# Splitting one projection of a slot around the values' transposes in a two-layer delta-rule attention kernel

## What is computed

```python
mixed = x @ W_qkv;  z = x @ W_z                    # 16 key heads, 32 value heads, 128 wide
mixed = silu(causal_conv4(mixed))                  # 4 taps per channel
q, k, v = split(mixed);  q, k = l2norm(q), l2norm(k)
def step(S, (qt, kt, vt, gt, bt)):                 # over 512 positions
    S = S * exp(gt)
    u = (vt - kt . S) * bt
    S = S + outer(kt, u)
    return S, qt . S
o = rms_norm(o) * silu(z)                          # second layer: gate first, then the norm
y = o @ W_out
```

## Time and profile before

| | |
|---|---|
| median of 3 runs | 4766.57 us (4763.95 to 4771.02) |
| the profiled execution, its own time | 4774.79 us |
| its span | 4773.0 us |
| PE busy | 4393.9 us, 32596 products |
| DVE busy | 3868.8 us |
| ACT busy | 3005.2 us |
| POOL busy | 1009.3 us |
| DMA, mean | 89 GB/s |

### The profile page before, as it was taken

How to read it: one execution, slowest core, us unless ns; L and a number is a source line. 1 busy time by engine, 2 the same in 40 slices (tenths; PEclk the granted TensorE clock), 3 DMA queues, 4 the chain that set the end, 5 groups by cost and what they waited for, 6 DMA issues and landing times. The chain is left out here.

```text
span 4773.0 us, 93590 instructions
## 1 busy us (share of the span) xinstructions
PE 4393.9 (92%) x32596; PEld 3619.4 (76%) x32596; DVE 3868.8 (81%) x8126; ACT 3005.2 (63%) x9834; POOL 1009.3 (21%) x1252
## 2 busy tenths in 40 slices
PE   5899948999999999999959999299999999999998
PEld 3578736888888888888845877288888888888887
DVE  5938987888888888888851599788888888888887
ACT  1146636777777777777721666267777776767675
POOL 0014421122221212212100344021212122221211
PEclk8999978999999999999979999599999999999999
DMA  1035642232222223223210556222322222322222
GB/s 57 16 96 172 185 129 87 83 85 77 83 80 83 80 78 83 78 82 89 65 31 7 148 176 194 88 80 81 86 77 80 77 83 77 83 79 83 73 83 66
DMA packets 580414, 422.57 MB, mean 89 GB/s; under 512 B 392808, under 2 KB 476312, under 8 KB 579502
## 3 DMA queue, kind: packets, MB, share of 16 engines
q1 hardware_dynamic: 563566, 408.20, 29.4%
q0 software_dynamic: 16384, 8.42, 1.0%
HBM read 296.24 MB, written 120.16 MB: 87 GB/s over the span
## 5 line engine op out<-in xcount | busy, mean ns | idle before, releaser
L1232 DVE SCALAR_TENSOR_TENSOR conv_l<-mix_l,taps_l,conv_l 128x512 f32<-128x512 f32 x1152 | 869.1, 764 | 62.7 <-ACT conv_l L1051 21.9
L854 PE MATMUL pj_l<-x_high,w_high_l 128*128 128x512 f32 x1280 | 574.5, 449 | 160.5 <-ACT w_high_l L1060 160.5
L1435 POOL TENSOR_TENSOR fac_l<-den_l,powers 128x4 f32<-128x4 f32 x256 | 258.5, 1012 | 1622.5 <-DVE den_l L1356 1621.1
L1198 ACT ACTIVATE Z_l<-gb_l 128x128 f32<-128x128 f32 x1024 | 266.6, 288 | 433.1 <-PE gb_l L1014 433.0
L854 PE MATMUL pj_l<-x_high,w_low_l 128*128 128x512 f32 x1280 | 519.7, 406 | 2.6
L854 PE MATMUL pj_l<-x_low,w_high_l 128*128 128x512 f32 x1280 | 514.0, 402 | 0.0
L637 POOL DMA_DIRECT2D own_dram<-key_kkS_l x512 | 296.0, 585 | 925.5 <-ACT key_kkS_l L509 915.2
L1023 PE MATMUL gb_l<-wo_l,gT_l 128*128 128x256 f32 x2048 | 480.0, 384 | 0.0
L1023 PEld LDWEIGHTS gb_l<-wo_l,gT_l 128*128 128x128 f32 x2048 | 372.6, 190 | 69.7 <-ACT Z_l L1198 25.6
L1366 DVE SCALAR_TENSOR_TENSOR x<-gb_l,fac_l,x 128x256 f32<-128x256 f32 x1024 | 412.9, 476 | 13.6 <-POOL fac_l L1435 4.0
L854 PEld LDWEIGHTS pj_l<-x_high,w_high_l 128*128 128x128 f32 x1280 | 243.2, 190 | 219.0 <-ACT w_high_l L1060 160.8
(11 more groups left out here) (204 smaller groups left out, 10588.5 us busy)
## 6 DMA issues: line engine op xcount, KB each, us to landing
rows_l<-rows_dram SPq DMA_DIRECT2D x128, 1024.0 KB, 5.6
k_dram<-kT_l SPq DMA_DIRECT2D x128, 256.0 KB, 2.3
kk_dram<-key_kkS_l SPq DMA_DIRECT2D x128, 256.0 KB, 2.4
kq_l<-k_dram SPq DMA_DIRECT2D x128, 256.0 KB, 3.3
kkS_l<-kk_dram SPq DMA_DIRECT2D x128, 256.0 KB, 5.9
w_raw_l<-in_wx SPq DMA_DIRECT2D x32, 640.0 KB
lane_k_l<-own_dram SPq DMA_DIRECT2D x32, 512.0 KB, 4.1
t_dram<-lane_t_l SPq DMA_DIRECT2D x14, 1024.0 KB, 4.9
```

The source lines that it names most:

```text
L854: ins = nc.tensor.matmul(pj_bank(c, t), wt[:, k, t, :], xt[:, k, :, at], start=(k == 0 and n == 0), stop=(k == KD - 1 and n == 2))
L1198: ins = nc.scalar.activation(Z[:, g, bank(b)], gb[:, 0, g, bank(b)], ACT.Square, accum_out=ss_o[:, g, b:b + 1])
L1232: ins = nc.vector.scalar_tensor_tensor(out, mix[:, t, :, i:i + P], wt(i), out, ALU.mult, ALU.add)
L1435: nc.gpsimd.tensor_tensor(fac[:, g, :], den[:, g, :], m.powers[:, 1, :], ALU.pow).then_inc(fac_ok[g], 1)
```

## The change

In each slot that has it, the second half (k = 1) of projection 0 moves from ahead of the values' transposes to behind them, ahead of the outputs' transposes. It is the same six products into the same bank. The prologue's projection (L1034, L1035) stays as it is.

```diff
                     if it < KHEADS * CHUNKS - 2:
                         project(*following(nh, ncn), 0, 0, False)
-                        project(*following(nh, ncn), 0, 1, False)
                     if not last:
                         values_token_major(nh, ncn)
+                    if it < KHEADS * CHUNKS - 2:
+                        project(*following(nh, ncn), 0, 1, False)
                     for g in range(GROUPS):
```

## The result

| | before | after |
|---|---|---|
| median, 5 runs each | 4769.52 us | 4793.64 us |
| lowest to highest | 4763.95 to 4771.02 | 4787.42 to 4795.86 |
| ratio, 95% interval | | 1.0050 [1.0039, 1.0062] |
| span of the profiled execution | 4773.0 | 4788.6 |

The kernel is slower by 24.1 us. I had forecast 21.9.

The account below looks back on a forecast made before the run. PE, 92% busy, was taken to set slot length except where it waits for DVE in c = 2. Terms +21.3 and +0.6 gave +21.9 us; on the 4766.57 base, 4788.5 us forecast, range 4777 to 4797.

Parts of the forecast that it names:

- c = 3: 30 slots, 15 per layer: V stays put, the half's 0.71 us is not hidden before the outputs' transposes; +21.3 us.
- c = 0 and c = 1: 64 slots: V arrives before the first half ends, so values start 0.71 us earlier and outputs start unchanged; cost 0.
- c = 2, second layer: V falls inside the second half, but the outputs' transposes wait 0.50 us for the first gate anyway; cost 0.
- c = 2, first layer: First group's outputs' transposes 0.51 us later, hidden by two covers; taken as 0, at most 15 x 0.51 = 7.7 us.
- the first cover: First layer: output projection still waits for its gate; late ACT squares (1557.59) just precede the product needing them (1557.70).
- The border: One extra entry into a projection per slot, 124 in all: 0.005 us each, +0.6 us; at most 3.7 us.
- The exposed weight load: Rival: each extra entry into a projection exposes a 0.19 us weight load, 23.6 us more, 4812 us; chance 0.03.
- The clock: Rival: PE's longer idle time in 30 slots drops its clock to 1.2 GHz, another 21 us, 4810 us; chance 0.01.

## Why the prediction was right

**What bounds the kernel, and c = 3.** Right. V did not move with PE, the wait ahead of the values grew to 0.86 us, the outputs came at 1.64 behind the values, and DVE, ACT and the next slots moved along. The term was 30 x 0.71 = 21.3 us; the table above gives 10.5 + 10.6 = 21.1 and the run with c = 3 alone 21.0.

**c = 0 and c = 1.** Right: 0.00 us in 64 slots.

**c = 2, second layer.** Right: the first gate still sets the start of the outputs' transposes (V + 1.69 after, V + 1.68 before), and V to V is unchanged.

**c = 2, first layer.** This term was mis-sized: I took 0 out of a range up to 7.7 us, and it is 3.5. The delays were as worked out (squares 0.49 us late, sums of x 0.33), and the first cover held: the output projection was not late. The step that failed is "DVE is some 0.3 to 0.5 us late into the c = 3 slot, where it has 0.91 us to wait anyway". The 0.91 us lie at L1252, 7 us behind the W blocks that PE takes from DVE first, and there PE had slack for only about half of the delay. By then ACT, which ends the wait at L1252, is late with PE: DVE comes 0.30 us later than before and still waits 0.83 us. I had asked where DVE would catch up and not who waits for it before that.

**The border.** Forecast 0.005 us each. From V to the outputs' transposes of c = 0 it is 0.007 us more than before in both layers, of c = 1 0.003 at most. The exposed weight load, which the rule of the Trainium skill that the prediction names would have given ("TensorE: Matmul & The Clock Gate", "Part 3: Packing small matmuls"), shows nowhere, so the trace does not agree with that rule here: 94 splits cost 4.0 us with 3.6 of them in c = 2 of the first layer, where 94 loads of 0.19 us would have made 17.9.

**The clock.** 1.00 in each of the four windows, 2.4 GHz, through slots with 0.86 us without a product; and 1.00 too over the stretches from 739 to 2360 us and from 3108 to 4773 us, in both profiles. The rival falls.

**What the profile was to show.** One mark of mine was wrong although the mechanism was right, and another was read from the wrong row. I had said that the window from the values of c = 3 to those of c = 0 would grow to 24.2 us; it is 23.49, because the values of c = 0 start 0.71 earlier in their own slot, and the window of c = 1 to c = 2 shows the growth instead (28.06), where I had allowed 0.1. And the idle time ahead of L894 grew by 73 us, not by 42. The 34.5 us that I took for idle weight loads are loads and products added up, and the view of waits has them apart (us, times, longest). Before, the products had 7.3 us in 2 waits, and the loads:

```profile
PEld kk_l L894 <- DVE ap_l L1287: 27.2, 62, 4.5
```

After:

```profile
PEld kk_l L894 <- DVE ap_l L1288: 67.7, 62, 3.4
PE kk_l L894 <- DVE ap_l L1288: 39.7, 62, 2.7
```

The loads' idle time grew by 40.5 us, about the 42 of the forecast, half of it in c = 2, where it costs nothing or little. The other 32.4 are the products' idle time ahead of the same transposes, which had not been printed before.

**The sum.** 21.9 us forecast, 24.1 measured. The missing 2.2 are the 3.5 of the first layer's c = 2, less 0.6 of borders and 0.2 of c = 3, to within half a us. The forecast of the time itself, 4788.5 us, is 5.1 under the measured 4793.64: 2.2 of the change, and 3.0 because the kernel before has a median of 4769.52 in five runs and had 4766.57 in the three that I took as the base. (The 4784 in the prediction's span of the forecast should be 4785, 4763.95 plus 21; the range does not hang on it.)

## What to carry to other kernels

Work that stands ahead of a wait is free exactly as far as it runs beside the wait. Before splitting it, mark the time at which the awaited event arrives and see whether it lies before or behind the point of the split: where the event is earlier, the second part costs nothing. Where the event is later than both parts, it costs its full length (0.71 us in c = 3), and where the event falls inside the second part, something less (the outputs' transposes 0.52 us late in the first layer's c = 2), unless a later wait covers it. To follow a delay on another engine, go through everything that others take from it in order, and stop at its idle time only after that. And to say which slot lost time after a reorder, measure between marks that the edit does not move.

## What the runs showed that I had not expected

A wait that PE's idle time doesn't show: in the slots with c = 3 of the kernel before, PE waits 0.15 us for V, and the list of PE's waits has none of them (its two entries for L894, 7.3 us, belong to the start of each layer, at 748.1 and 3082.5 us), since the modelled end of the last projection product (0.40 us, at a pitch of 0.235) covers it. With the first half alone ahead, 0.86 us without a start are printed as 0.70. Small waits behind long products are read from starts.

The largest gain of the study was not at the place of the change: 0.57 us of DVE waiting for ACT and 0.7 us of work that nobody needed yet, in 30 slots, were worth 25 us (0.5%), and moving them took the price of the change in the first layer's c = 2 away as well.
